# Four columns of layer 0 aggregate by seven block products and store their adjacency units for layer 1

## The chip, the cores and the metric

The kernel runs on one core of a Trainium2 chip. The metric is the device time in microseconds (us), the median of the runs. The core has five engines that matter here, each with its own in-order queue: TensorE (PE; its weight loads are shown apart as PEld), VectorE (DVE), ScalarE (ACT), GpSimd (POOL) and SyncE (SP), which issues most DMA transfers. They wait for each other by semaphores only.

## The reference, cut to what matters

Four graph layers on x (2708 x 512) with one adjacency matrix (2708 x 2708, float32), each of them pre-normalised and residual:

```python
# layer 0
h = jnp.maximum(_layernorm(x), 0.0)
deg = jnp.sum(adj, axis=1); dinv = (deg + 1.0) ** (-0.5)
x = x + relu(dinv[:, None] * (adj + eye) * dinv[None, :] @ h @ W0)
# layer 1
h = jnp.maximum(_layernorm(x), 0.0)
x = x + (dis[:, None] * adj * dis[None, :]) @ h @ W1.T + b1
# layer 2: as layer 0 with W2 (adj + eye);  layer 3: adj @ (h @ W) with sigmoid gates,
# and an attention over adj's non-zeros, which the kernel does as a fifth pass
```

Row and column scalings are folded into h and into the factors after the projection, so that what is multiplied is the raw adjacency, with ones added on the diagonal in layers 0 and 2 only.

## The kernel before, in words

**Tiling.** The aggregation computes (adj @ h) transposed. A pass p (0 to 3 for the layers, 4 for the attention) is cut into six columns of output nodes, numbered g = 6p + c in `CHUNKS`: c = 0 to 3 are 512 wide, c = 4 is 256 wide, c = 5 is 404 wide. Each column sums over 22 tiles j of 128 source nodes (tile 21 has 20 rows); j and j + 1 make a pair J = j // 2 for j below 20. `SEQ` is the order of all steps ("agg", g, j).

**Precision.** Every operand is a sum of a high and a low float16 half, and a product takes three matmuls (high x high, high x low, low x high). The halves of the adjacency are made on the way: a DMA brings a float32 tile of adjT, ScalarE writes the scaled high half (line 1826), VectorE the low half (line 1498). h's halves are made once per layer.

**Plain columns** (`g < GW`, here GW = 6, so all of layer 0; and pass 4) take 4 x 3 matmuls of the column's width for each j (lines 1246 to 1248), into four PSUM banks, and the other four banks take the projection by W.

**Columns of seven products** (`winograd(g)`: GW to GE - 1, layers 1 to 3) take a pair of tiles as a 2 x 2 block matrix with blocks of half the width, and h's pair as a 2 x 2 block matrix too. Instead of eight block products there are seven (Strassen-Winograd): 7 x 2 x 3 matmuls of half the width (lines 1199 to 1201), 24 of them at even j and 18 at odd j. They need sums of adjacency blocks (`sums`, GpSimd, lines 2020, 2023, 2025: T1 and T3, then T2, then T4), which are split like the rest (4 blocks at even j, 3 at odd j), and sums of h's blocks (`h_sums`, GpSimd, lines 2035 to 2040), of which HB holds seven images in high and low halves. Seven banks hold sums; one bank, "x", takes the projections one tile at a time (`spaced`). The end of such a column takes 1 ScalarE and 7 VectorE operations on PSUM (lines 1847, 1504, 1507, 1537) and a cast and a subtraction per block (1890, 1544), where a plain column takes four of each (1900, 1551).

**Units.** The split blocks of a pair lie together as a unit of 14 half widths in float16 (896 KB where the column is 512 wide; the two float32 tiles are 512 KB). Layer 1 makes its units and stores them in HBM (`a_keep`, issued by ScalarE, to `Ad`); layers 2 and 3 load them (`fly(g, j)` false), but for the pairs on the diagonal in layer 2. Eighteen of layer 1's units (`AHEAD`) are made during layer 0 already, beside its plain columns, in buffers of their own (`rt` and `pre`), and are loaded in layer 1.

**Head.** The first 24 or so steps of layer 0 run beside the row sums of adj (VectorE line 1375 and ScalarE line 1749), the moments of x, and h itself: ScalarE line 1767 and 1772, VectorE line 1465. `HEAD` interleaves the steps of columns 0 and 1.

**Transition to layer 1.** As column g of layer 0 has been projected, its tiles get the residual (`post`), moments, norm, `normed` (1786), `h_sums`, `hi` (1802), `lo` (1481), an image in HBM (`HBd`) and, when layer 0 no longer reads that pair's place in HB, a `restore` from it, here in two DMAs (slots 0 to 3, and 4 to 6, where slots 4 to 6 serve as scratch in layer 0). GpSimd adds layer 1's bias to x (`xbias`, line 2047).

**Order.** `schedule()` walks over SEQ and puts every stage into one list; each engine runs its part of that list in order. `plan(u, stage)` puts a stage at step u, `later(u, us)` finds the step that lies so many us later by a cost table, and `ahead(u)` issues fetches, sums and splits some steps before their use (at most `LA` = 4 steps for a split, 9 for a fetch). Buffers in U: five `raw` and five `sp` slots for plain tiles, three `rt` slots and four `un` slots for units.

```python
        while split < len(splits) and near(splits[split], u, LA, 10.4 if splits[split][1] >= GE else 9.6):
```

## Time and profile before

| | us |
|---|---|
| median of 3 runs | 1769.69 (1768.86 to 1770.41) |
| the profiled execution: span, first to last instruction | 1767.2 |
| its own time, around the span | not listed; the median of the runs is 2.5 above the span |

| engine | busy us | share |
|---|---|---|
| PE | 1694.0 | 96% |
| PEld | 1162.1 | 66% |
| DVE | 1115.5 | 63% |
| ACT | 773.1 | 44% |
| POOL | 616.1 | 35% |

The page's chain of work that ended last is 75% PE, 13% DVE, 5% DMA and 4% ACT. By TensorE's lines in order of time, layer 0's columns 0 and 1 end at 143.0 and 149.1 us, columns 2 to 5 at 220.0, 291.2, 336.4 and 390.5 us, layer 1's columns 6 to 11 at 459.7, 521.6, 584.5, 644.5, 675.9 and 733.4 us. "Busy" is time inside instructions; an idle engine that nobody waits for costs nothing.

### The profile page before, as it was taken

What the parts mean: (1) busy time and instruction counts of PE and PEld (TensorE: products, weight loads), DVE (VectorE), ACT (ScalarE), POOL (GpSimd) and SP (SyncE); (2) the same over time, 40 slices, a digit from 0 to 9 for tenths busy, and PEclk for the clock granted to TensorE, in tenths of its full rate; (3) what the DMA queues carried; (4) which work ended last, traced back from release to release, by engine and by line L of the source; (5) the groups of instructions that cost most, each with busy time, mean ns of one, the idle gap of its engine ahead of it and who ended that gap; (6) DMA issues with size and microseconds to landing.
All of it is one profiled execution on the core that took longest, in us unless ns stands there. A gap on an engine that the chain in (4) does not pass through costs nothing.

```text
span 1767.2 us, 31679 instructions
## 1 busy us (share of the span) xinstructions
PE 1694.0 (96%) x12862; PEld 1162.1 (66%) x12862; DVE 1115.5 (63%) x1941; ACT 773.1 (44%) x1176; POOL 616.1 (35%) x567
## 2 busy tenths in 40 slices
PE   3999998899899998999999999999999999999998
PEld 1444444657787887887887887788788544444445
DVE  5787888867868766533533445553651676777765
ACT  5675555544443343322322223210110568667655
POOL 0001656527656643420321111111200446455441
PEclk9999999999999999999999999999999999999999
DMA  9994788698777879976674879976655443443434
GB/s 391 361 341 150 267 316 291 213 353 288 280 262 276 328 248 331 311 265 228 220 238 130 287 248 313 355 247 232 210 152 175 134 127 99 149 138 113 144 95 133
DMA packets 185559, 417.08 MB, mean 236 GB/s; under 512 B 18340, under 2 KB 79136, under 8 KB 181680
## 3 DMA queue, kind: packets, MB, share of 16 engines
q1 hardware_dynamic: 151544, 337.14, 56.7%
q10 hardware_dynamic: 33868, 77.90, 11.7%
q8 instruction: 101, 1.65, 0.4%
q14 instruction: 46, 0.38, 0.1%
HBM read 303.80 MB, written 111.17 MB: 235 GB/s over the span
## 4 chain that ended last, share of the span: by engine, by line
PE 75%; DVE 13%; DMA 5%; ACT 4%; issue 1%; POOL 1%; SPq 0%; ACTq 0%; DVEq 0%; POOLq 0%
PE ps L1153 16%; PE ps L1199 11%; PE ps L1200 11%; PE ps L1201 11%; PE ps L1246 8%; PE ps L1247 8%; PE ps L1248 8%; DVE U L1498 4%; DMA U<-in_adjT 3%; ACT U L1826 1%; DVE CT L1537 1%; DMA U<-in_adj 1%; DVE OT L1544 1%; DVE stage L1481 1%; DVE HB L1498 1%
## 5 line engine op out<-in xcount | busy, mean ns | idle before, releaser
L1199 PE MATMUL ps<-U,HB 128*128 128x256 f16 (+2 forms) x2520 | 633.8, 260 | 8.2 <-DVE U L1498 3.7
L1200 PE MATMUL ps<-U,HB 128*128 128x256 f16 (+2 forms) x2520 | 633.6, 260 | 0.0
L1201 PE MATMUL ps<-U,HB 128*128 128x256 f16 (+2 forms) x2520 | 633.5, 260 | 0.0
L1246 PE MATMUL ps<-U,HB 128*128 128x512 f16 (+3 forms) x960 | 340.3, 357 | 20.5 <-DVE U L1498 13.9
L1247 PE MATMUL ps<-U,HB 128*128 128x512 f16 (+3 forms) x960 | 340.3, 357 | 0.0
L1248 PE MATMUL ps<-U,HB 128*128 128x512 f16 (+3 forms) x960 | 340.1, 357 | 0.0
L1498 DVE SCALAR_TENSOR_TENSOR U<-U,cS 128x512 f16<-128x512 f32 (+6 forms) x255 | 257.8, 1034 | 109.0 <-ACT U L1826 108.1
L1153 PE MATMUL ps<-W,OT 128*128 128x512 f16 (+1 forms) x1320 | 301.3, 382 | 9.9 <-DVE xr L1567 7.0
L1826 ACT ACTIVATE U<-U,cS 128x512 f16<-128x512 f32 (+6 forms) x255 | 199.3, 804 | 170.5 <-POOL U L2020 53.3
L1199 PEld LDWEIGHTS ps<-U,HB 128*128 128x128 f16 x2520 | 246.0, 98 | 38.8 <-DVE U L1498 5.8
L1200 PEld LDWEIGHTS ps<-U,HB 128*128 128x128 f16 x2520 | 246.2, 98 | 25.7
L1201 PEld LDWEIGHTS ps<-U,HB 128*128 128x128 f16 x2520 | 246.1, 98 | 19.2
L2066 POOL TENSOR_TENSOR U<-U 128x512 f32<-128x512 f32 (+2 forms) x126 | 173.9, 1380 | 183.5 <-DVE U L1518 182.8
L1153 PEld LDWEIGHTS ps<-W,OT 128*128 128x128 f16 (+1 forms) x1320 | 128.2, 98 | 155.7 <-DVE xr L1567 8.0
L1246 PEld LDWEIGHTS ps<-U,HB 128*128 128x128 f16 x960 | 94.8, 99 | 117.1 <-DVE U L1498 17.4
L2020 POOL TENSOR_TENSOR U<-U 128x512 f32<-128x512 f32 (+2 forms) x70 | 102.1, 1458 | 165.5 <-DMA U<-in_adjT 164.7
L1248 PEld LDWEIGHTS ps<-U,HB 128*128 128x128 f16 x960 | 94.7, 99 | 93.5 <-issue 2.8
L1247 PEld LDWEIGHTS ps<-U,HB 128*128 128x128 f16 x960 | 94.7, 99 | 89.8 <-issue 2.6
L1518 DVE SCALAR_TENSOR_TENSOR U<-U 128x512 f32<-128x512 f32 (+1 forms) x126 | 91.2, 724 | 64.0 <-ACT U L1863 57.7
L2035 POOL TENSOR_TENSOR Q<-Q 128x256 f32<-128x256 f32 x30 | 23.4, 779 | 301.3 <-ACT Q L1786 301.3
L1528 DVE TENSOR_TENSOR U<-U 128x512 f16<-128x512 f32 (+1 forms) x126 | 98.1, 780 | 40.5 <-ACT U L1882 40.1
L1856 ACT ACTIVATE U<-HB,SR 128x512 f32<-128x512 f32 (+2 forms) x132 | 87.9, 668 | 34.9 <-DVE U L1518 34.5
(207 smaller groups left out, 1889.6 us busy)
## 6 DMA issues: line engine op xcount, KB each, us to landing
U<-Ad SPq DMA_DIRECT2D x83, 896.0 KB, 6.5
U<-in_adjT SPq DMA_DIRECT2D x289, 256.0 KB, 4.4
Ad<-U ACTq DMA_DIRECT2D x35, 896.0 KB, 5.0
xd<-xr SPq DMA_DIRECT2D x84, 256.0 KB, 6.0
xr<-xd SPq DMA_DIRECT2D x84, 256.0 KB, 5.4
U<-in_adj SPq DMA_DIRECT2D x14, 1354.0 KB, 8.6
U<-Ad SPq DMA_DIRECT2D x23, 707.0 KB, 5.7
HBd<-stage ACTq DMA_DIRECT2D x16, 896.0 KB, 9.1
```

The source lines that it names most:

```text
L1153: last = eng.matmul(o, src(i, c), weight(k, c), start=n == 0 and c == 0, stop=n == 2 and c == 3)
L1199: eng.matmul(o, h[0], hi, start=J == 0 and a == 0, stop=False)
L1200: eng.matmul(o, h[0], lo, start=False, stop=False)
L1201: last = eng.matmul(o, h[1], hi, start=False, stop=to in "acg" and J == 9 and a == 1)
L1246: eng.matmul(o, h[0], hi, start=j == 0, stop=False)
L1247: eng.matmul(o, h[0], lo, start=False, stop=False)
L1248: last = eng.matmul(o, h[1], hi, start=False, stop=False)
L1498: eng.scalar_tensor_tensor(lo, unsplit(g, j), cS[:, n:n + 1], hi, ALU.mult, ALU.subtract).then_inc(s_slo, 1)
L1528: eng.tensor_tensor(lo, em[:, (e - 1) % 3, 0:w], hi, ALU.subtract).then_inc(s_elo, 1)
L1826: eng.mul(split_of(g, j)[0], unsplit(g, j), cS[0:r, n:n + 1]).then_inc(s_shi, 1)
L2020: eng.tensor_tensor(unit[:, T1:T3 + 1, :], unit[:, T4:A22 + 1:2, :], unit[:, A11:T4 + 1, :], ALU.subtract).then_inc(s_tsum, 1)
L2066: eng.tensor_tensor(acc[0:r, g % 2, 0:w], acc[0:r, g % 2, 0:w], em[0:r, (e - 1) % 3, 0:w], ALU.add).then_inc(s_acc, 1)
```

## The change

Columns 2 to 5 of layer 0 become columns of seven products: GW goes from 6 to 2. So h of layer 0 needs its block sums and their halves too, for all eleven pairs. The units of columns 2 to 5 are stored, and columns 8 to 11 of layer 1 load them; only the pairs on the diagonal (where layer 0 adds ones and layer 1 does not) are made again there. Columns 6 and 7 are made in layer 1, all ten pairs each. `AHEAD`, its buffers and its 18 units are gone. Layer 2 and 3 load from where a unit without ones was stored first.

Two of the four weight images are made later (`WCOL`): w1 stays in column 3, w2 moves from column 4 to 9, w3 from column 2 to 10; the gate weights go from column 2 to 8. Their scratch is a buffer of its own (`wtmp`) instead of HB's slots; HB's slots 4 to 6 now hold h's sums in layer 0, so a restore is one DMA. h's block H21, which has no place in HB, lies in CT and bias during columns 0 and 1.

```diff
-GW = 6
+GW = 2
+WCOL = {1: 3, 2: 9, 3: 10, 4: W4}
+GCOL = 8
-AHEAD = [(g, j) for g in range(GW, 12) for j in
-         ((0, 2, 4) if g == 6 else (0, 2) if g == 8 else (0, 2, 10) if g < 11 else (0, 2, 8, 14))]
+def selfloops(g):
+    return g // 6 % 2 == 0 and g < GE
+def diagonal_unit(g, j):
+    return on_diagonal(g, j) or j < 20 and on_diagonal(g, j ^ 1)
 def fly(g, j):
-    if g < 12:
-        return not made_ahead(g, j)
-    return g < 18 and (on_diagonal(g, j) or j < 20 and on_diagonal(g, j ^ 1)) or g >= GE
+    return g < 8 or g < 18 and diagonal_unit(g, j) or g >= GE
+def kept(g, j):
+    return GW <= g < 12 and fly(g, j) and j == whole(j) and not (selfloops(g) and diagonal_unit(g, j))
+def keeper(g, j):
+    return g % 6 + (6 if g % 6 < GW or diagonal_unit(g, j) else 0)
...
         for i, t in enumerate(tiles(g)):
-            post(later(u + 1, 2.6 * i), p, t)
+            post(u + 1 + i // 2 if g == 0 else later(u + 1, 2.6 * i), p, t)
...
-        at_us = {0: (6.5, 9.5, 12.5, 15.5) if now == GW else (8, 11.5, 15, 18.5), ...
+        at_us = {0: (6.5, 9.5, 12.5, 15.5) if now == 6 else ..., 2: (12, 18.5, 36.5, 41.5) if now == GW else ...
...
         if 3 <= i < NT + 3:
-            put("h", 0, i - 3)
+            t = i - 3
+            put("h", 0, t)
+            if t % 2:
+                put("h_sums", 0, t // 2)
+            elif t:
+                put("s_hi", t // 2 - 1)
+                put("s_lo", t // 2 - 1)
+        if i == NT + 3:
+            put("s_hi", 10)
+            put("s_lo", 10)
...
+                elif kind == "s_lo":                                  # VectorE
+                    J, = of
+                    dve.wait_ge(s_phi, J + 1)
+                    if J < 10:
+                        eng.tensor_tensor(HB[:, S1:S4 + 1, J, 1, :], Q[:, S1:S4 + 1, :], HB[:, S1:S4 + 1, J, 0, :],
+                                          ALU.subtract).then_inc(s_hslo, 1)
...
                 elif kind == "h":                                     # ScalarE
-                    act.wait_ge(s_hlo, t - 1)
+                    act.wait_ge(s_hlo, t - 1 if t < 20 else t)
+                    if t % 2 == 0 and t < 20:
+                        act.wait_ge(s_ssum, 2 * J)
+                    else:
+                        act.wait_ge(s_hsum, J if t < 20 else 10)
...
-                        a, b = plain_slots(t)
-                        eng.copy(HB[:, a:b + 1:b - a, t // 2, 0, :], q).then_inc(s_hhi, 1)
+                        for hi, whole_of in plain_parts(t, 0):
+                            last = eng.copy(hi, whole_of)
+                        last.then_inc(s_hhi, 1)
...
+                elif kind == "s_hi":                                  # ScalarE
+                    J, = of
+                    act.wait_ge(s_hsum, s("h_sums", 0, J))
+                    if J < 10:
+                        eng.copy(HB[:, S1:S4 + 1, J, 0, :], Q[:, S1:S4 + 1, :]).then_inc(s_phi, 1)
...
                 elif kind == "h_sums":                                # GpSimd
+                    if l == 0:
+                        pool.wait_ge(s_hslo, J)
...
                 elif kind == "restore":                               # SyncE
-                    l, J, a, b = of
-                    if l == 1 and b == 7:
-                        sync.wait_ge(s_wlo, 4)
-                        sync.wait_ge(s_wkept, 48)
-                        sync.wait_ge(*KEPT[[key for key in AHEAD if LANE[("pre",) + key] == 7][-1]])
+                    l, J = of
...
                 elif kind == "constants":
+                    sync.wait_ge(s_agg, s("agg", 1, 19))
```

`plain_parts` writes an even tile's two halves in two instructions of 256 elements where one of 512 stood, since H21 lies elsewhere; an odd tile keeps one. The DMA descriptor scratch is cut to 256 bytes, which makes room for `wtmp`.

## Rows read from the trace of the kernel before

**Rows 1.** Windows: length, busy us PE PEld DVE ACT POOL, clock, DMA share, GB/s.

```profile
45.00:143.00 98.00, 96.45 (x439) 43.52 (x440) 73.80 (x191) 68.39 (x96) 3.89 (x7) 0.98 0.86 315
149.00:220.00 71.00, 68.08 (x310) 30.63 (x309) 58.71 (x81) 36.28 (x49) 38.47 (x34) 0.98 0.69 235
220.00:291.00 71.00, 66.32 (x307) 29.61 (x305) 61.03 (x72) 39.05 (x52) 46.09 (x38) 1.00 0.81 295
291.00:336.00 45.00, 40.51 (x306) 30.36 (x304) 38.83 (x72) 25.90 (x46) 16.50 (x21) 0.96 0.74 248
336.00:390.00 54.00, 54.00 (x307) 29.80 (x305) 36.54 (x62) 26.52 (x43) 23.52 (x25) 1.00 0.92 318
390.00:460.00 70.00, 66.34 (x532) 51.38 (x530) 50.69 (x71) 31.47 (x41) 44.34 (x37) 1.00 0.84 298
460.00:521.60 61.60, 59.95 (x500) 48.40 (x498) 41.85 (x56) 23.52 (x28) 30.73 (x27) 1.00 0.76 279
521.60:733.40 211.80, 202.57 (x1979) 169.22 (x1977) 150.30 (x207) 87.86 (x111) 120.40 (x121) 0.99 0.81 289
794.60:854.30 59.70, 59.70 (x503) 48.91 (x501) 22.66 (x44) 14.61 (x20) 4.18 (x6) 1.00 0.62 214
973.70:1004.90 31.20, 30.63 (x479) 27.62 (x477) 13.38 (x21) 7.47 (x11) 3.99 (x8) 1.00 0.85 278
```

**Rows 2.** Waits of TensorE from 149 to 390 us: total us, times, longest.

```profile
PE ps L1246 <- DVE U L1498: 12.1, 8, 2.9
```

**Rows 3.** Waits of TensorE from 390 to 734 us.

```profile
PE ps L1153 <- DVE xr L1567: 7.0, 4, 3.2
...
PE ps L1214 <- DVE ht L1478: 2.1, 1, 2.1
```

**Rows 4.** Timeline of TensorE at 60 us: start us, length.

```profile
59.99 0.38 PE L1246 MATMUL ps<-U,HB 128*128 128x512 f16 x1
...
60.85 0.38 PE L1247 MATMUL ps<-U,HB 128*128 128x512 f16 x1
```

**Rows 5.** Timeline of TensorE at 855 us.

```profile
855.03 0.27 PE L1201 MATMUL ps<-U,HB 128*128 128x256 f16 x1
...
855.90 0.27 PE L1200 MATMUL ps<-U,HB 128*128 128x256 f16 x1
```

**Rows 6.** Waits of all engines from 50 to 133 us.

```profile
ACT Q L1767 <- DVE NB L1445: 15.1, 7, 2.2
DVE HB L1465 <- ACT HB L1772: 10.1, 7, 1.6
...
ACT U L1826 <- PE ps L1248: 4.0, 5, 1.9
```

**Rows 7.** VectorE groups, 45 to 143 us: busy us, mean ns, idle before.

```profile
L1498 DVE SCALAR_TENSOR_TENSOR U<-U,cS 128x512 f16<-128x512 f32 x36 | 26.1, 762 | 3.8 <-ACT U L1826 3.8
L1465 DVE TENSOR_TENSOR HB<-Q,HB 128x512 f16<-128x512 f32 x15 | 10.1, 675 | 10.1 <-ACT HB L1772 10.1
```

**Rows 8.** VectorE groups by form, 149 to 390 us.

```profile
L1498 DVE SCALAR_TENSOR_TENSOR U<-U,cS 128x512 f16<-128x512 f32 x42 | 40.6, 980 | 19.5 <-ACT U L1826 19.5
L1481 DVE TENSOR_TENSOR stage<-Q,stage 128x1792 f16<-128x1792 f32 x8 | 18.3, 2282 | 0.5 <-ACT stage L1802 0.5
L1498 DVE SCALAR_TENSOR_TENSOR U<-U,cS 128x768 f16<-128x768 f32 x6 | 10.0, 1672 | 0.0
L1596 DVE SCALAR_TENSOR_TENSOR HB<-HB,wS 128x2048 f16<-128x2048 f32 x3 | 7.2, 2409 | 0.0
L1498 DVE SCALAR_TENSOR_TENSOR U<-U,cS 128x808 f16<-128x808 f32 x2 | 2.1, 1056 | 0.4 <-ACT U L1826 0.4
```

**Rows 9.** GpSimd groups by form, 149 to 390 us.

```profile
L2020 POOL TENSOR_TENSOR U<-U 128x512 f32<-128x512 f32 x11 | 16.9, 1532 | 23.3 <-DMA U<-in_adjT 23.3
```

**Rows 10.** GpSimd line 2020 over the span: duration min/median/max ns.

```profile
L2020 POOL TENSOR_TENSOR U<-U x70: 725/1271/3202, 158.1 to 1027.8; 128x512 f32<-128x512 f32 x48, 128x256 f32<-128x256 f32 x11, 128x404 f32<-128x404 f32 x11
```

**Rows 11.** GpSimd line 2035 over the span: duration min/median/max ns.

```profile
L2035 POOL TENSOR_TENSOR Q<-Q x30: 717/727/1731, 180.3 to 1091.0; 128x256 f32<-128x256 f32 x30
```

More of the change, by code:

```diff
@@ L37 @@
 NRAW = 5
-NEXTRA = 3
 NSP = 5
@@ L273, in schedule @@
     scores = [k for k in splits if k[1] >= GE]
-    eyes = [k for k in splits if on_diagonal(*k[1:]) and (k[1] < GW or 12 <= k[1] < GE and k[2] >= 20)]
+    eyes = [k for k in splits if on_diagonal(*k[1:]) and selfloops(k[1]) and (k[1] < GW or k[2] >= 20)]
     def plan(u, *stage):
@@ L317, in ahead @@
             g, j = splits[split][1:]
-            if not have(("fetch", "agg", g, j)) or splits[split] in eyes and not have(("eye", g, j)) or g < 2 and not have(("scale", g)) or g >= GE and not have(("mask", g, j)):
+            if not have(("fetch", "agg", g, j)) or splits[split] in eyes and not have(("eye", g, j)) or not have(("scale", min(g, 2))) or g >= GE and not have(("mask", g, j)):
                 break
@@ L529, in schedule @@
     plan(AT["agg", 5, 18], "factors", 1)
-    plan(AT["agg", 6, 15], "factors", 2)
+    plan(AT["agg", 11, 15], "factors", 2)
     plan(AT["agg", W4, 18], "factors", 3)
-    for n, (g, j) in enumerate(AHEAD):
-        u = later(AT["agg", 2, 1], 7.8 * n)
-        for us, *stage in ((0, "fetch", "pre", g, j), (0, "fetch", "pre", g, j + 1), (7.5, "sums", g, j),
-                           (11, "split", g, j), (12, "split", g, j + 1), (17, "a_keep", g, j)):
-            plan(later(u, us), *stage)
     for _, g, j in SEQ:
-        if GW <= g < 12 and j == whole(j) and fly(g, j):
+        if kept(g, j):
             plan(AT["agg", g, j], "a_keep", g, j)
```

209 lines of the change are left out of this document (105 added, 104 removed).

## The prediction

> **What bounds the kernel now.** I read the page first (busy shares), then the windows cut at the ends of the columns, then TensorE's waits, then the groups of VectorE and GpSimd by form. The page says that TensorE is busy for 96% of the span. The windows show that this isn't so evenly: the loss up to 45 us apart, what is missing lies in layers 0 and 1. In columns 2 to 5 TensorE is idle for 12.1 us, in eight waits, all for VectorE's split of the adjacency [rows 2]; VectorE is busy for 58.7 of 71, 61.0 of 71, 38.8 of 45 and 36.5 of 54 us there, 195 of 241 in all, and GpSimd 124.6 [rows 1]. From 390 to 733 us, 343.4 us long, TensorE is busy for 328.9 [rows 1], so 14.5 us are missing; 7.0 of them are waits for VectorE's residual addition that frees the projection's bank, 2.1 for h's last pair [rows 3]. A column of layer 2 shows what is left when the units come ready from HBM: 59.7 us long, 59.7 busy, VectorE 22.7, GpSimd 4.2 [rows 1]. So TensorE's work is the bound, and where it stalls, VectorE with GpSimd beside it is. The change takes from the first and gives to the second.
>
> **TensorE's work.** A matmul of 512 columns starts every 0.215 us (0.86 over four) [rows 4], one of 256 every 0.109 (0.87 over eight) [rows 5]. A pair costs 24 x 0.215 = 5.16 us plain and 42 x 0.109 = 4.58 by seven products: 0.6 saved. Tiles 20 and 21 cost the same (24 and 8 half-width matmuls for 12 and 4). Ten pairs and widths 512 + 512 + 256 + 404 = 1684, so 3.29 x 6.0 = **19.7 us less**. This is on the path wherever TensorE isn't idle. Projections don't change, they only move: column 1's four go from column 3 into column 2, two of column 4's from column 6 into column 5; each is 12 x 0.215 = 2.6 us. The floor of the new columns 2 to 5 is then 59.7 + 10.3 = 70, 59.7, 31.2 (the 256-wide column of layer 2 [rows 1]) and about 49.7 (59.7 with its 49.3 us of pairs scaled to 404): 210.7 us, against 241.5 now; column 6's is 59.7 against 69.2.
>
> **Work for VectorE and GpSimd in columns 2 to 5.** Durations undisturbed: 512 elements 0.76 us [rows 7], 808 elements 1.056 [rows 8], so 1024 about 1.27 and 768 about 1.01; a 512-wide unit costs VectorE 2.28 us, a 256-wide 1.4, a 404-wide 1.9. On GpSimd 1.27 for 512 elements [rows 10] and 0.73 for 256 [rows 11]: 2.73 for a 512-wide unit, 1.65 and 2.2 (estimates) for the others.
> Instructions of VectorE with both operands in SBUF: now 84 plain splits (about 56 us), 18 units ahead (37), eight `lo` of 2.0 (16): 107 us. After: 40 units 45.6 + 14 + 19 = 79, single tiles 3, `lo` 16, the subtractions of three column ends 7: 105. No change there. The rest of VectorE, some 60 us now: two weight images leave (each 2.4 us for the low half [rows 8], as much for the maximum, some 0.8 besides: -11), the gate weights -1.6, three plain column ends -6.4, three new ones with seven PSUM operations +12.5, two more residuals and moments +2.7: about 57.
> GpSimd now: 18 units 44, 16 bias additions 20, eight pairs of sums 23, ones on the diagonal 6: 93 us undisturbed. After: 40 units 55 + 16.5 + 22 = 93, bias 20, pairs 23, ones 6: **142 us**. This is the term that grows.
> The two disturb each other. The same split of 512 elements takes 0.762 us in the head, where GpSimd is idle, and 0.980 in columns 2 to 5 [rows 7, 8]; 768 elements take 1.67 instead of 1.01 [rows 8]; GpSimd's T1 and T3 take 1.53 instead of 1.27 [rows 9, 10]. Measured busy minus undisturbed is about 29 us for VectorE and 32 for GpSimd in the 241 us, where by their shares (135 and 125 of 241) they lay beside each other for 70: nearly 0.87 us lost per us of overlap. So what both do adds up almost as on one resource: now 107 + 93 = 200 less 0.13 x 70 = 191 of 241 us (79%). After, 105 + 142 = 247, less 0.13 x 150 (all that can overlap), is 228, against a floor of 210.7. At 97% filling that is **233 us, 8 less than now**, of which TensorE idles 22.
> The bounds: 213 if the overlap were free, 256 if it gave nothing (247 / 0.97).
>
> The Trainium skill, page "SBUF — State Buffer", section "Who interferes with whom", says that a VectorE instruction with two SBUF inputs and a GpSimd instruction that reads SBUF contend for one read interface, which is locked for a whole instruction, not shared. The rows here agree with the contention and nearly with the lock; by the lock alone the stretch would be 247 us or more, and this is the slower rival below.
>
> **The head.** Per pair of tiles (10.4 us of TensorE) ScalarE gets a cast of 1024 elements (about 1.05) and 0.2 for the split-up copy, VectorE a subtraction of 1024 (2 x 0.675 [rows 7] less the fixed part: 1.2) and 0.15, GpSimd 4 x 0.73 [rows 11]. VectorE goes from 73.8 to some 87 of 98 us, and to 94 with what GpSimd's 29 us cost it. The two engines work hand in hand there: ScalarE waited 15.1 us for the norm factors, VectorE 10.1 for the cast of h, and ScalarE for TensorE only 4.0 in 83 us [rows 6]. So TensorE's pace holds with little to spare: some 6 to 8 us of splits made ahead, and the 4.0. I take 1.6 us more per pair on that alternation, 16 in all, less 9 of slack: **+7 us**. Bounds: 0 (all in the gaps: 24 us of VectorE) and +18. If the cover goes, the steps of columns 0 and 1 wait for their splits.
>
> **Columns 6 to 11.** Column 6 makes ten units instead of seven; VectorE 50.7 + 7 + 3 in 60, GpSimd 44 + 8. DMA: its share was 0.92 in column 5 and 0.84 in column 6 [rows 1]; column 5 gets nine stores of a 404-wide unit (6.5 MB) for the 54 us' 17.2 MB less 2.7 MB, column 6 three units more, 4.3 MB. At 2.8 us per MB that is about 121 us of DMA for both, whose floor is 109. I take 65 for column 6: **-4** against 69.2 (bounds -9.5 and +3). Column 7: -0.5. Columns 8 to 11, 211.8 us now [rows 1], load 33 units; VectorE's 150 us and GpSimd's 120 shrink by 26 units (59 and 70 us) and get two weight images (+11). Floor 59.7 + 59.7 + 31.2 + 49.7 = 200; I take 203: **-9**, since the waits for the residual addition [rows 3] go when its queue is short. Bounds -11 and -2 (transfers of x).
> At nothing: the single `restore` (same bytes, same step; the pair's place frees no earlier), the bias load behind step (1, 19) on SP (planned after it anyway; behind it stand fetches whose slots aren't free before), ScalarE's stores (61 for 60), the weights' scratch. In layers 2 and 3 nothing changes.
>
> **The sum.** +7 - 8 - 4 - 0.5 - 9 = -15 (the 19.7 saved and some 9 us of present waits removed, less 14 of new ones). Span 1767.2 - 15 = 1752; the median of the runs lies 2.5 above the span: **1755 us**.
>
> **Rivals.**
> (1) *The pair of engines gives the whole gain back.* Place: columns 2 to 6. With no gain from overlap 2 to 5 take 250 to 256 instead of 241, column 6 +2, the head loses 12 or more by the same disturbance, 8 to 11 still gain 9: +14, 1784 us. It decides once VectorE's and GpSimd's joint work passes some 240 us in columns 2 to 5, 15 us above my 233 less friction. For: 0.87 lost per us; stretches where TensorE waited had VectorE at 86% [rows 1, 2]. Against: VectorE reached no more than 86% over a column, and still lost only 4.7 us of 71.
> (2) *It fits.* Head +2, columns 2 to 5 at 213 (-28), 6 at 60 (-9), 7 at 60 (-1.6), 8 to 11 at 201 (-11): -47, 1722 us. For: layer 1's columns with seven or eight units made in a column lose under 3 us [rows 1]. Against: GpSimd 142 of 211 us undisturbed, 185 disturbed.
> (3) *A draw.* The head's alternation is on TensorE's path in full (+16), the rest as forecast: 1764; with DMA holding column 6 at 70 also 1769. Within 0.2% of now. For: ScalarE's 4.0 us in 83.
> That the stored units aren't read can be left out: columns 8 to 11 name them by `keeper`.
>
> **How the numbers follow.** Forecast 0.45, its own range 1746 to 1765; rival 1 0.25; rival 2 0.18; rival 3 0.12. A measurement here tells 0.2% (3.5 us) from no change. Faster: forecast, rival 2 and a little of 3: 0.64. Same: the rest of 3 and the upper edge of the forecast's terms: 0.11. Slower: rival 1: 0.25. The range stops short of both outer rivals' prices, since half of each of their chances lies nearer: 1732 to 1785.
>
> **What would show it.** Right: matmuls in columns 2 to 5 of the half width at 0.109; these columns 225 to 240 us long, waits for the splits there of about 20 us (12.1 now), GpSimd over 80% busy; the head's end at 153 to 160 us instead of 149; columns 8 to 11 near 203 with hardly a wait for the residual. Wrong: a head unchanged at 149 (rival 2's side), or columns 2 to 5 over 241; a split's mean in columns 2 to 5 near the undisturbed 1.27 and 1.01 would break the contention term; a slower layer 2 or 3 would mean a cause not seen here.

## The result, and the profile after

| | before | after |
|---|---|---|
| median of 4 runs each, in turn on one chip | 1770.05 us (1768.86 to 1770.51) | 1817.76 us (1816.77 to 1819.21) |
| ratio | | 1.0272, 95% interval 1.0258 to 1.0287 |
| span of the profiled execution | 1767.2 us | 1815.6 us |
| mean granted clock | 0.994 | 0.981 |

The change costs 48 us; the forecast was 1755. Each stretch below runs from one column's last step to the next one's, on TensorE's records (differences are taken before rounding):

| stretch | before | forecast | after | after less before |
|---|---|---|---|---|
| head (columns 0, 1), end | 149.1 | 156 | 178.9 | +29.8 |
| columns 2 to 5 | 241.4 | 233 | 254.7 | +13.2 |
| column 6 | 69.2 | 65 | 79.0 | +9.8 |
| column 7 | 61.9 | 61.4 | 66.3 | +4.4 |
| columns 8 to 11 | 211.8 | 203 | 204.3 | -7.5 |

Over the forecast the head is 22.8 us, columns 2 to 5 21.7, column 6 14.0, column 7 4.9 and columns 8 to 11 1.3. From column 12 on the kernels differ by under 3 us. The page of the changed kernel, its part on busy time:

```profile
PE 1692.4 (93%) x13646; PEld 1221.3 (67%) x13646; DVE 1099.0 (61%) x1917; ACT 748.3 (41%) x1129; POOL 667.2 (37%) x627
```

TensorE's busy time was 1694.0 before. It fell by 1.6 us where 19.7 us of matmuls went away, and what it isn't busy rose from 73.2 to 123.2. So +50.0 - 1.6 = +48.4 us, the whole difference of the spans, and 18.1 us of busy time more than the work accounts for. Most of them are matmuls at the lower of the clock's two levels, 1.2 GHz: by the traces' record of the granted clock, TensorE was busy for 49.8 us at that level, against 20.2 before, and a 512-wide matmul started every 0.427 us there instead of every 0.216. Half of the 29.6 us more is 14.8 (an estimate from these figures); where the other 3 us lie is open. The windows of the changed kernel (columns as in [rows 1]), first two stretches of the head, then columns 2 to 7 one by one, 8 to 11 together and one of layer 2:

```profile
45.00:143.00 98.00, 88.92 (x396) 39.37 (x397) 80.77 (x177) 68.36 (x99) 29.62 (x32) 0.97 0.87 315
143.00:179.00 36.00, 20.01 (x71) 7.48 (x69) 19.14 (x44) 16.99 (x27) 11.41 (x13) 0.76 0.14 45
179.00:255.00 76.00, 72.53 (x549) 54.25 (x550) 59.62 (x72) 35.15 (x43) 65.08 (x54) 0.96 0.66 232
255.00:333.00 78.00, 65.84 (x504) 50.55 (x502) 59.01 (x77) 36.79 (x44) 53.45 (x51) 0.93 0.68 237
333.00:371.20 38.20, 33.46 (x478) 29.26 (x476) 27.12 (x39) 17.85 (x28) 25.85 (x33) 0.91 0.73 246
371.20:433.60 62.40, 53.31 (x503) 45.81 (x503) 48.65 (x68) 31.22 (x43) 41.82 (x47) 0.95 0.90 318
433.60:512.60 79.00, 63.97 (x502) 49.26 (x501) 61.81 (x76) 36.27 (x45) 60.30 (x47) 0.94 0.80 282
512.60:578.90 66.30, 62.06 (x502) 49.30 (x501) 43.73 (x63) 27.23 (x32) 37.27 (x33) 0.97 0.85 306
578.90:783.20 204.30, 200.55 (x1984) 170.15 (x1983) 99.13 (x183) 50.53 (x64) 40.62 (x52) 1.00 0.75 261
844.40:904.20 59.80, 59.80 (x503) 49.00 (x502) 22.74 (x45) 14.62 (x20) 4.31 (x7) 1.00 0.62 215
```

The reader is to see three things. From 143 to 179 us TensorE works for 20 of 36 us, and no other engine is near its limit: VectorE 19.1, ScalarE 17.0, GpSimd 11.4, DMA share 0.14. That is not a lack of capacity. In columns 3, 4, 5 and 6 TensorE is busy for 81 to 88%, at a clock of 0.91 to 0.95, while VectorE is busy for 71 to 78%. And columns 8 to 11, where the stored units are read, run almost without a gap. TensorE's waits, first from 179 to 434 us, then from 434 to 784:

```profile
PE ps L1153 <- DVE xr L1573: 13.3, 4, 5.4
PE ps L1199 <- DVE U L1510: 5.3, 2, 2.9
PE ps L1199 <- DVE xr L1573: 3.7, 1, 3.7
```

```profile
PE ps L1153 <- DVE xr L1573: 8.7, 2, 7.3
PE ps L1199 <- DVE U L1510: 6.2, 2, 3.5
PE ps L1179 <- DVE xr L1579: 3.2, 1, 3.2
```

Before, the waits of columns 2 to 5 were all for splits [rows 2]; now the residual addition (L1573), which gives the projection its one bank back, is the larger part.

**The end of the head.** GpSimd's timeline (start us, length, then in brackets the idle time before it and what ended it):

```profile
144.43 0.51 POOL L2021 PARTITION_ALL_REDUCE wm<-wm  x1 [7.70 <-DVE wm L1595]
146.67 0.35 POOL L2018 PARTITION_ALL_REDUCE cm<-cm  x1 [1.73 <-DVE cm L1385]
155.15 0.71 POOL L2067 TENSOR_TENSOR Q<-Q 128x256 f32<-128x256 f32 x1 [8.14 <-issue]
...
164.13 0.38 POOL L2024 PARTITION_ALL_REDUCE wm<-wm  x1 [6.09 <-issue]
171.47 0.72 POOL L2061 TENSOR_TENSOR Q<-Q 128x256 f32<-128x256 f32 x1 [6.97 <-issue]
```

"issue" says that GpSimd waited for nothing that the profile shows. It stands so 6.1 us ahead of an all-reduce that follows an addition, and 8.1 and 7.0 us ahead of an addition that follows an all-reduce; between two all-reduces it doesn't. The ten traces of changed kernels that keep the all-reduces (e4's is left aside) show the same three gaps: 5.8 to 6.1 us ahead of the all-reduce, 6.7 to 8.8 us behind one. The Trainium skill, page "GPSIMD Engine Reference", section "Instruction dispatch", says that the first call to a freshly loaded GpSimd kernel pays a load of about 6 us that no instruction of the profile shows. The gap of 6.09 us has that length, but no run shows that it is this load; the way back takes 7 to 8 us here. The gap isn't unrecorded work of the all-reduce itself, since VectorE had the result of the one at 146.67 at once, and the addition at 155.15 came 8.1 us later:

```profile
147.05 0.15 DVE L1329 TENSOR_SCALAR cm<-cm 128x1 f32<-128x1 f32 x1 [0.49 <-POOL cm L2018]
```

VectorE and TensorE over the same stretch of the changed kernel:

```profile
DVE wm L1329 <- POOL wm L2024: 11.6, 1, 11.6
```

```profile
166.15 0.58 PE L1249 MATMUL ps<-U,h 128*128 128x512 f16 x1 [9.80 <-DVE h L1470]
```

VectorE stands 11.6 us in `degrees` for the all-reduce at 164.1, with h(20) behind it in order, and TensorE stands 9.8 us for h(20). In the kernel before the same three all-reduces come together, and no one asks GpSimd for anything until 152.7:

```profile
128.62 0.76 POOL L1991 PARTITION_ALL_REDUCE wm<-wm  x1 [65.39 <-DVE wm L1583]
131.11 0.35 POOL L1988 PARTITION_ALL_REDUCE cm<-cm  x1 [1.73 <-DVE cm L1382]
137.45 0.35 POOL L1994 PARTITION_ALL_REDUCE wm<-wm  x1 [5.98 <-DVE wm L1407]
152.71 0.76 POOL L2003 TENSOR_TENSOR U<-U,identf 128x128 f32<-128x128 f32 x1 [14.91 <-DMA U<-in_adjT]
```

**The middle of the head.** VectorE's groups from 45 to 143 us (answering [rows 7]), then ScalarE's and VectorE's waits from 50 to 133 ([rows 6]):

```profile
L1510 DVE SCALAR_TENSOR_TENSOR U<-U,cS 128x512 f16<-128x512 f32 x32 | 28.1, 926 | 3.4 <-ACT U L1857 3.3
L1478 DVE TENSOR_TENSOR HB<-Q,HB 128x1024 f16<-128x1024 f32 x8 | 9.7, 1219 | 0.0
...
L1467 DVE TENSOR_TENSOR HB<-Q,HB 128x512 f16<-128x512 f32 x7 | 5.0, 708 | 9.8 <-ACT HB L1791 9.8
```

```profile
ACT Q L1786 <- DVE NB L1448: 18.3, 6, 3.4
DVE HB L1467 <- ACT HB L1791: 8.1, 5, 1.6
```

The split of 512 elements takes 926 ns instead of 762. By the starts of h of the even tiles on ScalarE a pair takes 12.7 us from 87 to 138 us, against 10.4 to 10.5 before, and ScalarE's wait for the norm factors grows from 15.1 to 18.3 us: it is VectorE that is late.

### The profile page after: what moved, and what is told of

It is laid out like the page before. It is cut to its first block, busy times and chain, and to the rows that moved or that the text cites. A ratio compares the mean times of both kernels' runs of the same rounds, so it can differ in the third digit from the quotient of the medians.

```text
span 1815.6 us, 33148 instructions
## 1 busy us (share of the span) xinstructions
PE 1692.4 (93%) x13646; PEld 1221.3 (67%) x13646; DVE 1099.0 (61%) x1917; ACT 748.3 (41%) x1129; POOL 667.2 (37%) x627
## 3 DMA queue, kind: packets, MB, share of 16 engines
q10 hardware_dynamic: 33868, 77.90, 11.3%
## 4 chain that ended last, share of the span: by engine, by line
PE 69%; DVE 13%; DMA 6%; ACT 4%; POOL 4%; issue 3%; SPq 1%; ACTq 0%; DVEq 0%; POOLq 0%
PE ps L1153 14%; PE ps L1199 12%; PE ps L1200 12%; PE ps L1201 12%; PE ps L1249 5%; PE ps L1250 5%; PE ps L1251 5%; DMA U<-in_adjT 4%; DVE U L1510 4%; DVE CT L1549 2%; ACT U L1857 1%; DMA xr<-xd 1%; POOL U L2050 1%; DVE bn L1424 1%; POOL xr L2079 1%
## 5 line engine op out<-in xcount | busy, mean ns | idle before, releaser
L1199 PE MATMUL ps<-U,HB 128*128 128x256 f16 (+2 forms) x3080 | 774.1, 260 | 22.7 <-DVE U L1510 12.6
L1200 PE MATMUL ps<-U,HB 128*128 128x256 f16 (+2 forms) x3080 | 773.5, 260 | 0.0
L1201 PE MATMUL ps<-U,HB 128*128 128x256 f16 (+2 forms) x3080 | 773.4, 260 | 0.0
L1199 PEld LDWEIGHTS ps<-U,HB 128*128 128x128 f16 x3080 | 302.4, 98 | 61.1 <-DVE U L1510 18.4
L1153 PE MATMUL ps<-W,OT 128*128 128x512 f16 (+1 forms) x1320 | 308.2, 387 | 28.2 <-DVE xr L1573 22.0
L1200 PEld LDWEIGHTS ps<-U,HB 128*128 128x128 f16 x3080 | 302.9, 98 | 31.7 <-issue 0.3
L1201 PEld LDWEIGHTS ps<-U,HB 128*128 128x128 f16 x3080 | 302.6, 98 | 23.1
L1510 DVE SCALAR_TENSOR_TENSOR U<-U,cS 128x512 f16<-128x512 f32 (+5 forms) x202 | 230.7, 1172 | 88.9 <-ACT U L1857 87.9
L1249 PE MATMUL ps<-U,HB 128*128 128x512 f16 (+1 forms) x600 | 214.7, 362 | 21.4 <-DVE HB L1467 8.3
L1857 ACT ACTIVATE U<-U,cS 128x512 f16<-128x512 f32 (+5 forms) x202 | 173.4, 889 | 142.2 <-POOL U L2050 84.6
L1250 PE MATMUL ps<-U,HB 128*128 128x512 f16 (+1 forms) x600 | 214.5, 362 | 0.0
L1251 PE MATMUL ps<-U,HB 128*128 128x512 f16 (+1 forms) x600 | 214.4, 362 | 0.0
L2067 POOL TENSOR_TENSOR Q<-Q 128x256 f32<-128x256 f32 x40 | 33.2, 831 | 453.5 <-ACT Q L1817 376.4
L1249 PEld LDWEIGHTS ps<-U,HB 128*128 128x128 f16 x600 | 59.1, 99 | 86.4 <-issue 21.6
L1251 PEld LDWEIGHTS ps<-U,HB 128*128 128x128 f16 x600 | 59.1, 99 | 62.7 <-issue 2.4
L1250 PEld LDWEIGHTS ps<-U,HB 128*128 128x128 f16 x600 | 59.1, 99 | 59.0 <-issue 1.9
```

The costliest lines, as they stand in the source:

```text
L1153: last = eng.matmul(o, src(i, c), weight(k, c), start=n == 0 and c == 0, stop=n == 2 and c == 3)
L1199: eng.matmul(o, h[0], hi, start=J == 0 and a == 0, stop=False)
L1200: eng.matmul(o, h[0], lo, start=False, stop=False)
L1201: last = eng.matmul(o, h[1], hi, start=False, stop=to in "acg" and J == 9 and a == 1)
L1249: eng.matmul(o, h[0], hi, start=j == 0, stop=False)
L1250: eng.matmul(o, h[0], lo, start=False, stop=False)
```

## The experiments

Each run was timed in turn with the kernel before on the same chip; the changed kernel's ratio of 1.0272 is what to compare with. "Columns 3 to 7" took 323.8 us in the changed kernel.

**1. e1_no_allreduce** (the three of L2018, L2021, L2024 alike):

```
-  eng.partition_all_reduce(wm[:, 1, 6:7], wm[:, 0, 6:7], P, RMAX)
+  eng.tensor_copy(wm[:, 1, 6:7], wm[:, 0, 6:7])
```

> The changed kernel with its three partition all-reduces on GpSimd (L2018, L2021, L2024) replaced by plain copies of one column; it leaves out the maximum over the partitions. Theory A (GpSimd stands 6 to 8 us each time it goes from its elementwise additions to an all-reduce and back, and the head's sums of h now make that switch in the middle of the head, where h(20) on ScalarE and the degree step on VectorE wait for it): the gaps of 8.1, 6.1 and 7.0 us behind and ahead of these instructions go, the head (columns 0 and 1) ends at 159 to 163 us instead of 178.9, and the time falls by 14 to 20 us, to 1798 to 1804. Rival B (the head is long because of the alternation of ScalarE and VectorE over h, its sums and the splits; GpSimd only fills the wait): the head ends within 4 us of 178.9 and the time stays within 1813 to 1819.

Measured: 1808.3 us, ratio 1.0209 (1.0178 to 1.0241), about 11 us less than the changed kernel; its profiled execution has a span of 1801.4, 14 less. The head ends at 167.7. GpSimd's timeline of this kernel:

```profile
146.14 0.18 POOL L2018 COPY cm<-cm 128x1 f32<-128x1 f32 x1 [1.89 <-DVE cm L1385]
146.90 0.73 POOL L2067 TENSOR_TENSOR Q<-Q 128x256 f32<-128x256 f32 x1 [0.57 <-ACT Q L1786]
...
153.13 0.18 POOL L2024 COPY wm<-wm 128x1 f32<-128x1 f32 x1 [1.95 <-DVE wm L1410]
```

The gaps are gone. Theory A holds in kind, but its sizes were too large: 11 us (14 by the spans) of its 14 to 20, and a head 4.7 us longer than its 163. The head kept 18.6 us more than before.

**2. e2_before_no_allreduce**: the same edit in the kernel before.

> The same replacement in the kernel before: three all-reduces on GpSimd become copies of one column, the maximum over the partitions is left out. Theory A: in the kernel before the three stand together at 128 to 137 us and nothing asks for GpSimd until 152 us, so the switches are hidden: the time stays within 3 us of 1770 (1767 to 1772). Rival B': the switches cost in the kernel before as well, and then the two kernels are to be compared without them: 1755 to 1765.

Measured: 1768.5 us, ratio 0.9996 (0.9979 to 1.0014). The three cost nothing there, as theory A says. GpSimd's timeline of this run:

```profile
138.51 0.18 POOL L1994 COPY wm<-wm 128x1 f32<-128x1 f32 x1 [6.16 <-DVE wm L1407]
153.64 0.93 POOL L2003 TENSOR_TENSOR U<-U,identf 128x128 f32<-128x128 f32 x1 [14.94 <-DMA U<-in_adjT]
```

The gaps of 5.98 and 14.91 us stay without the all-reduces, at 6.16 and 14.94. So they really were waits for VectorE and for a DMA, and the trace of before hides what a switch costs behind them.

**3. f1_head_sums_narrow**: on top of e1,

```
-  eng.tensor_tensor(Q[:, S1, :], Q[:, H21, :], Q[:, H22, :], ALU.add)
+  c = slice(0, 256 if l else 16)
+  eng.tensor_tensor(Q[:, S1, c], Q[:, H21, c], Q[:, H22, c], ALU.add)
   ... (S3, S2, S4 alike)
```

> The changed kernel without the all-reduces, as in e1_no_allreduce, and with the head's four sums of h on GpSimd computed on 16 of 256 columns of each block (the other columns stay zero, so these sums are left out); ScalarE's and VectorE's instructions stay whole. In e1_no_allreduce the head still ended at 167.7 us, 18.6 us after that of the kernel before. Theory A (those 18.6 us are mostly GpSimd's additions against VectorE: the splits take 1021 ns beside them instead of 746, and h of the next even tile waits for the sums): the cycle of a pair falls from 12.7 us to 11.2 to 11.8 us, the head ends at 157 to 161 us and the time is 7 to 11 us below e1_no_allreduce (1797 to 1801). Rival B (ScalarE's s_hi, 1.04 us, and its two short copies for one long, with VectorE's s_lo, 1.22 us, carry it, which stay here): the head ends within 3 us of 167.7 and the time within 3 us of 1808.

Measured: 1794.4 us, ratio 1.0143 (1.0128 to 1.0158); the head ends at 158.0 and a pair takes 11.5 us. VectorE's splits from 80 to 128 us, first in e1, then here:

```profile
L1510 DVE SCALAR_TENSOR_TENSOR U<-U,cS 128x512 f16<-128x512 f32 x15 | 14.7, 1021 | 0.0
```

```profile
L1510 DVE SCALAR_TENSOR_TENSOR U<-U,cS 128x512 f16<-128x512 f32 x17 | 12.0, 746 | 1.4 <-ACT U L1857 1.4
```

Theory A: head and pair lie in its ranges; the median is 14 us under e1's and so 3 us under its range, the span 9.3 (1792.1). So 9.7 us of the head are GpSimd's additions beside VectorE.

**4. e3_s_hi_early**: `put("s_hi", J - 1)` ahead of `put("h", 0, t)` of the even tile.

> The changed kernel with ScalarE's copy of the upper halves of pair J-1's sums put ahead of h of the next even tile, where ScalarE now waits 3.4 us for NB, instead of behind it; nothing is left out. Theory A (the head runs in a cycle of 12.7 us a pair in which this copy, 1.04 us, stands between h and the splits on ScalarE): the cycle falls to 11.7 us, eight pairs give 5 to 8 us, less where the end of the head is set by GpSimd's stall, so the head ends at 172 to 177 and the time is 1810 to 1816. Rival B (the cycle is set by VectorE's splits beside GpSimd, not by ScalarE): the cycle stays 12.6 to 12.8 us and the time within 2 us of 1818.

Measured: 1816.9 us, ratio 1.0257 (1.0220 to 1.0293); a pair takes 12.6 us. Rival B: ScalarE's copy lies in time in which ScalarE waits for VectorE anyway (a new wait of 2.0 us a pair for GpSimd's sums took the place of the one for NB).

**5. f4_repaired**: maxima by way of DRAM, s_hi early, and the bias early:

```
+  eng.dma_start(mxd.rearrange("k p -> p k"), mx[:, 0:3]).then_inc(s_call, 16)
+  sync.wait_ge(s_call, 16)
+  eng.dma_start(mxb, <mxd as one row>.to_broadcast([P, 3 * P])).then_inc(s_call, 16)
   ...
+  eng.reduce_max(mx[:, 3:6], mxb[:, :, :], AX)   # VectorE, two steps later
```

> The changed kernel with nothing left out and three repairs: the three maxima over the partitions go through DRAM (one store of three columns and one broadcast load on SP, one reduction on VectorE two steps later) instead of three all-reduces on GpSimd; ScalarE's copy of the upper halves of the sums stands ahead of h of the next even tile; and the bias is added ahead of the sums of h. Theory A (all-reduce switches 10 to 14 us as in e1_no_allreduce, s_hi 1 to 3 us, bias 6 to 12 us, which add up as they lie in different stretches): 1791 to 1802, still slower than before (1769). Rival B (SP stands for the round trip through DRAM and its fetches come late, or the gains overlap): 1802 to 1812.

Measured: 1820.0 us, ratio 1.0278 (1.0262 to 1.0293), head to 182.5: worse than both theories. VectorE's timeline:

```profile
155.17 0.74 DVE L1532 SCALAR_TENSOR_TENSOR U<-U,cS 128x512 f16<-128x512 f32 x1
165.12 0.55 DVE L1431 TENSOR_REDUCE mx<-mxb 128x3 f32<-128x384 f32 x1 [9.20 <-DMA mxb<-mxd]
```

The store took 7.7 us to land and the load 5.6, 13.4 us from the store's issue. I had put a new wait where the old one was, with h(21) behind it.

**6. g4_maxima_behind_h**: the reduction and what hangs on it moved behind the last tile of h; the bias as in the change.

> The changed kernel with nothing left out: the three maxima through DRAM as in f4_repaired, but VectorE's reduction of them put behind the last tile of h, and ScalarE's copy of the sums' upper halves ahead of h of the next even tile; the bias is added where the change has it. In f4_repaired the round trip took 7.7 and 5.6 us and VectorE stood 9.2 us for it with h(21) behind. Theory A: the head ends at 163 to 168 us as in e1_no_allreduce, of which column 2 gives back up to 5 us waiting for its scale; time 1804 to 1811. Rival B (column 2 gives back all of it, since its first splits need that scale and come at 166 us either way): 1813 to 1819.

Measured: 1813.7 us, ratio 1.0236 (1.0221 to 1.0251). The head ends at 170.8 instead of 178.9, and column 2 takes 78.7 instead of 76.2. The time is in B's range and the mechanism is neither: the head gained 8.1 us where A has 11 or more, and column 2 gave back 2.5, where B has all of it. Of the repairs with nothing left out it is the one that can be told from the changed kernel.

**7. e4_no_bias**: `xbias` and SP's wait for it taken out.

> The changed kernel without the addition of the bias b1 on GpSimd (L2079) and without the wait for it ahead of the x_keep on SP; it leaves out that bias. Theory A (columns 2 to 7 are held by a loop: the fetches of adjT stand on SP behind an x_keep that waits for this addition, the addition stands on GpSimd behind tile pair sums that wait for fetches): columns 2 to 7 take 320 to 385 us instead of 400, and the time is 1798 to 1808. Rival B (the loop is closed by the three slots for fetched tiles and VectorE's splits, so GpSimd's and SP's order does not matter): columns 2 to 7 within 4 us of 400, time 1813 to 1819.

Measured: 1805.7 us, ratio 1.0192 (1.0160 to 1.0223), in A's range. Its profiled execution took 5637 us, three times the others, and isn't read, so the fall of columns 2 to 7 that A rests on isn't shown. Which part of the edit gave it, the next run narrows down.

**8. f2_bias_early**: the order only:

```
-  steps += [(5 if J < 9 else 9, "xbias", 2 * J), ...]
+  steps[2:2] = [(1.2, "xbias", 2 * J), ...]
```

> The changed kernel with nothing left out and one order changed: GpSimd adds the bias b1 to x ahead of the sums of h of the same pair (1.2 us after the norm in the plan) instead of behind them (5 us), so the x_keep on SP meets it done. Theory A (the loop SP, GpSimd, VectorE is opened at this wait; e4_no_bias gave 12 us): SP's wait for L2079 falls from 58 us to under 15 us and the time is 1806 to 1812. Rival B (what e4_no_bias gave is GpSimd's own time for 22 additions, 33 us, and their contention with VectorE, which stay here): SP waits less but columns 2 to 7 stay within 3 us of 400 and the time is 1815 to 1819.

Measured: 1817.8 us, ratio 1.0268 (1.0251 to 1.0285). SP's waits from 179 to 579 us, first in the changed kernel, then here:

```profile
SPq L1057 <- DVE U L1510: 214.2, 49, 38.4
SPq L607 <- POOL xr L2079: 58.5, 15, 14.0
```

```profile
SPq L1057 <- DVE U L1510: 262.2, 54, 38.3
...
SPq L607 <- POOL xr L2079: 3.3, 3, 1.7
```

Rival B in all its points: 55.2 us of the wait for the bias went and 48.0 came back as waits for a free slot one line on, and columns 2 to 7 took 398.4 us. The order of `x_keep` was not the cause, though its wait was the most striking row of the trace; what is left for e4's 12 us is GpSimd's own time, or VectorE's beside it, which no run parts.

**9. f3_four_fetch_slots**: four slots for fetched tiles, three for units.

> The changed kernel with the seven slots of U shared out in columns 2 to 7 as four for fetched tile pairs and three for finished units instead of three and four; nothing is left out. Theory A (three slots give a unit 3 x 6.0 = 18 us from fetch to finished split, and in column 3 it takes 7.8 us of fetch, 1.9 of wait, 3.5 of sums and 8.1 of splits, 21.3 us in all): a fourth slot gives 24 us, SP waits less for free slots, and columns 2 to 7 fall by 6 to 15 us, time 1803 to 1812. Rival B (the slots for finished units were the scarce ones, 8 us of splits and 8.9 us ahead of use and 6 us of use out of 24): with three of them the splits come later and columns 2 to 7 rise by 5 to 20 us, time 1823 to 1838. Rival C (neither; SP's wait ahead of x_keep is what delays fetches): within 3 us of 1818.

Measured: 1822.4 us, ratio 1.0292 (1.0276 to 1.0309). Column 5 fell from 62.4 to 55.2 us, column 6 rose from 79.0 to 83.1, column 7 from 66.3 to 68.3, columns 8 to 11 from 204.3 to 207.4. The time lies between C's range and B's; what is won in column 5 with the fourth fetch slot is lost in the columns behind it, where a slot for units is missing.

**10. g1_unit_sums_narrow and 11. g2_low_halves_narrow**, columns 3 to 7 only:

```
+  c = slice(0, 16 if 3 <= g < 8 else part[T2].shape[-1])      # g1, on L2053, L2055
+  c = slice(0, lo.shape[-1] // (4 if 3 <= g < 8 else 1))      # g2, on L1510
```

> The changed kernel with the second and third addition of every tile pair's sums on GpSimd (L2053, L2055, 1.5 and 1.3 us beside VectorE) computed on 16 of 256 columns in columns 3 to 7; the rest of these two blocks is left as it was, so it is left out of the result. Theory A (in columns 3 to 7 everything stands in line behind GpSimd: its unit sums hold up its sums of h, on which ScalarE's copy and, behind it in order, the splits and the residual wait; GpSimd's and VectorE's time together set the pace): columns 3 to 7 fall from 323.8 us to 285 to 305 (at TensorE's full pace they would be near 262) and the time to 1799 to 1810. Rival B (the pace is set by the fetches of adjT, 7 to 10 us each beside the stores and the traffic of x, not by GpSimd): within 4 us of 1818.

> The changed kernel with VectorE's half of every split (L1510) in columns 3 to 7 computed on a quarter of its columns, 0.4 to 0.6 us instead of 1.1 to 1.6 us; the other low halves are left out. VectorE's load in these columns falls by some 80 us. Theory A (GpSimd's queue and the waits in order behind it set the pace; VectorE waits 58.7 us for ScalarE's splits there as it is): the columns fall by 0 to 12 us, and less than in g1_unit_sums_narrow; time 1806 to 1818. Rival B (VectorE is the bound, 75 per cent busy, and GpSimd matters only by slowing it): the columns fall by 20 to 40 us, more than in g1_unit_sums_narrow; time 1778 to 1798.

Measured: g1 1805.9 us, ratio 1.0186 (1.0163 to 1.0209), columns 3 to 7 304.7 us (-19.1). g2 1798.8 us, ratio 1.0155 (1.0140 to 1.0170), the same columns 301.3 us (-22.5). GpSimd's groups from 255 to 580 us, changed kernel and g2:

```profile
L2079 POOL TENSOR_TENSOR xr<-xr,bias 128x512 f32<-128x512 f32 x17 | 31.1, 1850 | 0.0
L2053 POOL TENSOR_TENSOR U<-U 128x256 f32<-128x256 f32 x27 | 28.4, 1052 | 2.1
```

```profile
L2080 POOL TENSOR_TENSOR xr<-xr,bias 128x512 f32<-128x512 f32 x17 | 22.7, 1356 | 0.0
L2054 POOL TENSOR_TENSOR U<-U 128x256 f32<-128x256 f32 x28 | 21.0, 748 | 2.2
```

With the lighter VectorE these two groups of GpSimd's are 27 and 29% shorter, though nothing in them changed; the two other groups of its unit sums, of 256 and 512 elements, are 17 and 8% shorter. In columns 3 to 7 g1 took 48 us of busy time from GpSimd and VectorE's fell by 16 with it; g2 took 66 from VectorE and GpSimd's fell by 37. The gain is about the same, so I read the two not as two candidates for a bound but as one. g1 lies in A's range. g2 is its rival B's: the columns are in B's range, the time 0.8 us above it, and A's sentence that it would give less than g1 was wrong.

**12. g3_h_copies_later**: `(9, "hi")`, `(10.5, "lo")` for layer 1's pairs below 7.

> The changed kernel with nothing left out and ScalarE's and VectorE's copies of layer 1's h (L1833, L1493) put 4 us later behind GpSimd's sums of h (9 and 10.5 us after the norms in the plan instead of 5 and 6.5), for the pairs of columns 2 to 7, so that the splits and the residual stand in line ahead of them. Theory A (what costs is the wait in order: ScalarE stood 5.0 us for GpSimd's sums at 276 us, and the residual and TensorE's projection behind it came 3.3 us late): ScalarE's wait at L1833 goes, columns 2 to 7 fall by 4 to 12 us and the time to 1806 to 1814. Rival B (GpSimd's total time is what counts, and the wait only moves to the next instruction): within 3 us of 1818.

Measured: 1822.0 us, ratio 1.0291 (1.0272 to 1.0309). Rival B, and a us beyond it. ScalarE's wait for GpSimd's sums ahead of this copy fell from 12.0 to 5.8 us, and TensorE's for the residual went from 22.0 to 23.9: the wait only moved.

**13. h1_splits_less_ahead and 14. i1_splits_more_ahead**: 7.0 and 12.2 us instead of 9.6 in `ahead`.

> The changed kernel with nothing left out and the splits of columns 3 to 7 put into the order 7.0 us ahead of their use instead of 9.6, so that residuals, whose projections wait for the one free bank, stand ahead of splits whose tiles have not arrived. Theory A (the 20 us in which TensorE waits for L1573 come from the order: at 378.4 us in g2_low_halves_narrow ScalarE stood 5.1 us for a split and the residual's Relu came right behind it): that wait falls by 8 to 16 us, columns 3 to 7 by 5 to 15 us (323.8 before), time 1803 to 1813. Rival B (the tiles come late in themselves, and what is gained at the residual is lost at the splits, which now have 2.6 us less slack): within 4 us of 1818.

> The changed kernel with nothing left out and the splits of columns 3 to 7 put into the order 12.2 us ahead of their use instead of 9.6; h1_splits_less_ahead, with 7.0, took 11.8 us more than the changed kernel, against its expectation. Theory A (slack of a split against late tiles is what is short, so more of it gives back a part of what less of it took): TensorE's wait for L1510 in columns 3 to 7 falls from 11.5 us to under 6 and the time to 1808 to 1815. Rival B (9.6 us lies at the optimum: further ahead the residuals stand behind more splits whose tiles have not come, and the slots for finished units are held longer): 1818 to 1832.

Measured: h1 1829.6 us, ratio 1.0338 (1.0318 to 1.0359); i1 1817.7 us, ratio 1.0277 (1.0258 to 1.0296). TensorE's waits in columns 3 to 7, h1 and i1:

```profile
PE ps L1199 <- DVE U L1510: 21.9, 9, 8.4
PE ps L1153 <- DVE xr L1573: 19.7, 6, 7.8
```

```profile
PE ps L1153 <- DVE xr L1573: 19.6, 5, 6.8
PE ps L1199 <- DVE U L1510: 11.5, 4, 3.5
```

h1 goes against both of its cases: the wait for the residual fell by 2.3 us (22.0 in the changed kernel) and that for the splits rose by 10.4 (11.5 there), 12 us in all. i1's time is 0.3 us under B's range, and the wait for the splits stayed at 11.5, so A is out. Less ahead costs, further ahead changes nothing.

**15. h2_quarter_stores**: layer 0's stores of units cut to a quarter.

> The changed kernel with only the first quarter of each finished unit of columns 2 to 5 stored to DRAM (layer 1 reads that quarter four times over, so its adjacency is wrong there); some 25 MB of the 65 MB that the DMA engines move in these columns are left out, GpSimd, VectorE and ScalarE do all their work. Theory A (the tiles of adjT come 7 to 10 us after their fetch because the engines are shared with these stores, DMA share 0.66 to 0.91): the fetches of columns 3 to 5 land in 4 to 6 us, columns 2 to 5 fall from 254.7 to 230 to 245 us, and columns 6 and 7, which store nothing of this kind, stay; time 1803 to 1810. Rival B (GpSimd's and VectorE's pace sets it, the fetch time is only the wait for a slot that comes free late): columns 2 to 5 within 4 us, time 1814 to 1820.

Measured: 1812.0 us, ratio 1.0242 (1.0226 to 1.0258). The DMA share in column 3 fell from 0.68 to 0.51, columns 2 to 5 only from 254.7 to 249.9 us. 4.8 us in the columns is just beyond B's 4 and far from A's 10 to 25, and the time lies between their ranges: the stores are a small part.

**16. h3_light_side_engines**: e1, f1, e4, g1 and g2 at once.

> The changed kernel with everything that the other runs took from GpSimd and VectorE taken at once: no all-reduces, the head's sums of h on 16 columns, the unit sums' second and third addition on 16 columns and VectorE's halves of the splits on a quarter in columns 3 to 7, no bias; all of these are left out of the result. Theory A (the load of GpSimd and VectorE, with what stands in line behind it, is the whole distance to the forecast of 1755): the parts give 24, 19, 22 and 12 us, of which those of columns 3 to 7 overlap, so the head ends near 158, columns 3 to 7 take 265 to 285 us instead of 323.8 and the time is 1745 to 1765. Rival B (the DMA share of 0.9 in columns 5 to 7 and the late tiles stay and take it back): columns 3 to 7 take 290 to 300 us and the time is 1768 to 1780.

Measured: 1766.6 us, ratio 0.9983 (0.9969 to 0.9997). Its stretches against the forecast's: head 159.5 (156), columns 2 to 5 233.4 (233), column 6 73.0 (65), column 7 60.8 (61.4), 8 to 11 205.2 (203). Columns 3 to 7 took 290.8 us. The time is 1.6 us above A's range and 1.4 under B's, the columns are B's. So the forecast's columns but the sixth are reached only with far lighter side engines than it counted with: GpSimd was busy for 119 us in columns 2 to 5, where the forecast had 142 before any contention. Even then the whole gain over the kernel before is 3 us. TensorE's largest wait from 234 to 530 us:

```profile
PE ps L1148 <- DVE xr L1569: 15.3, 4, 9.3
```

The longest of the four, 9.3 us, is column 6's. ScalarE stood 11.3 us up to 419 us for GpSimd's sums, which waited for a tile of adjT; the residual's Relu stood behind it. Why that fetch was so late I did not settle.

**17. h4_repaired_less_ahead and 18. i2_repaired_more_ahead**: g4 with each of the two.

> g4_maxima_behind_h with the splits of columns 3 to 7 put 7.0 us ahead as in h1_splits_less_ahead; nothing is left out. If the two repairs add: g4_maxima_behind_h gave 4 us, h1 by theory A 5 to 15 us, time 1799 to 1809; by rival B 1810 to 1817. In either case slower than the kernel before (1770).

> g4_maxima_behind_h (1813.7) with the splits of columns 3 to 7 put 12.2 us ahead. Theory A: 1804 to 1811, the best version with nothing left out, but slower than the kernel before. Rival B: 1814 to 1828.

Measured: h4 1826.1 us, ratio 1.0330 (1.0307 to 1.0353), against both of its cases, since it has h1's 12 us; i2 1813.1 us, ratio 1.0244 (1.0222 to 1.0266), between its two cases and the same as g4. No version with nothing left out comes near the kernel before.

## Why the prediction was wrong, point by point

**The arithmetic (-19.7)** was right in its paces: at the full clock a matmul of 256 columns starts every 0.109 us and one of 512 every 0.216. **Columns 8 to 11 (-9; -7.5)** came nearly as forecast: with their units ready, columns 8 and 9 took 59.9 us each, where the floor was 59.7.

**The head (+7; +29.8 measured)** is the largest miss. It has three parts. The switches of GpSimd, 11.2 us (e1), were not in the sum, nor in the bounds of 0 and +18: the step listed what was added to each engine, but not what GpSimd's new additions would stand between. No row of before gave their price: the gaps around the all-reduces there were other engines' (e2). GpSimd's additions beside VectorE, 9.7 us (f1), were priced: "to 94 with what GpSimd's 29 us cost it". The prediction then set them against VectorE's share of the stretch, not against the alternation, where VectorE's work stands in TensorE's path because ScalarE waits for it. The rest, 158.0 - 149.1 = 8.9, looks like the forecast's +7, but that is luck in part: the 1.6 us more a pair was measured as 2.3 with contention and 1.1 without, so of ten pairs' 11 us only some 2 were found as slack, not 9.

**Columns 2 to 5 (-8; +13.2).** The loads were right, and the contention was no worse than forecast: GpSimd was expected at 142 us undisturbed and was busy for 186 (185 was named), VectorE's 105 + 57 = 162 grew to 194.4. That is 76 us lost; reckoned as the prediction did, from VectorE's 137.4 us with both operands in SBUF and GpSimd's 186.2 by their shares of 254.6, over an overlap of 100, so 0.76 us per us, where it had 0.87. By the trace at least one of the two was at such work for 226 us, and the forecast had 228. The step that failed is "At 97% filling". The same joint work took 254.7 us, a filling of 89%. The 97% came from no row: before, 191 of 241 us were filled, 79%. (228 / 0.97 is also 235, not 233.) A reason that fits: before, splits could be made far ahead of plain columns from a ring of eight fetched tiles; now each split hangs on a sum on GpSimd that hangs on a fetch that hangs on a slot that hangs on an older split, and the residual stands in the same line. f2, f3, g3, h1 and i1 show that no single link of this ring that they moved is the cause, and g1 and g2 that lighter work on either engine speeds it up; the ring as a whole was not tested against anything else. The Trainium skill, page "SBUF — State Buffer", section "Who interferes with whom", calls the shared interface an exclusive lock. The measured 0.76 us per us of overlap agrees with a strong contention and is short of a full lock, by which the joint work would have been 247 us and not 226.

**Column 6 (-4; +9.8) and column 7 (-0.5; +4.4).** The forecast read column 6 by its DMA share. Its terms for columns 5 and 6 (17.2 + 3.8 + 20.9 + 4.3 MB at 2.8 us) add up to 129 us and not to 121; by the measured shares it was 119 of 141 us, so the two columns are 22 us longer than their DMA. g1 and g2 gave column 6 3.2 and 5.7 us, column 7 4.6 and 5.5, so these belong to the same ring, with ten units to make in column 6 where seven were before.

**The clock** had no term. About 15 us of the 48.4 are matmuls at the lower level of the granted clock, which fell to 0.91 to 0.97 in the stretches with many short waits and to 0.76 in the head's end; before, it stood at 0.96 to 1.00 [rows 1]. A wait costs more than its length.

**At nothing.** Layers 2 and 3 cost nothing, as said: columns 12 to 17 are equal to 0.1 us, column 18 has 1.3 us more. The restores, the order of SP's bias load and the later image loads were not tested by themselves.

**The rivals.** Rival 1, given 0.25, was right in its place, and its 250 to 256 us for columns 2 to 5 came true, but by luck: it had no gain from overlap and 97% filling, and the runs show a gain of 0.24 us per us and 89%. Its point of decision, a joint work of some 240 us, was not reached. Its head of +12 and its 1784 us were too low, so the range ended at 1785 and 1818 lies outside it. Rival 3 had the head's alternation in full, at +16; that term was measured as 18.6, without the switches.

**What would have shown it.** Of the forecast's own signs, "columns 2 to 5 over 241" did, and so did the head's end and GpSimd, busy for 73% instead of over 80. TensorE's waits there were for the residual (18.7 us) and not, as it said, for the splits (5.3). The split means bore the contention term out: 1024 elements took 1.50 us and 768 1.36, where 1.27 and 1.01 were undisturbed.
